# Two conv-style attention layers on one core: heads in pairs, one per half of the matrix rows, and maxima carried in freed position rows

## What is computed

```python
attn = jnp.einsum('bqd,bkd->bqk', q * scale, k)
rel_h = jnp.einsum('bhwc,hkc->bhwk', rq, Rh)
rel_w = jnp.einsum('bhwc,wkc->bhwk', rq, Rw)
attn = attn.reshape(...) + rel_h[..., :, None] + rel_w[..., None, :]
attn = jax.nn.softmax(attn.reshape(Bn * nh, Hh * Ww, Hh * Ww), axis=-1)
out = attn @ v          # then the heads side by side, @ wo + bo
```

## Time and profile before

| what | value |
|---|---|
| runs | 84.46 us median of 3 (84.38 to 84.9) |
| the profiled execution | 84.41 us, its span 82.7 us |
| busy: PE, PEld, DVE, ACT, POOL | 75.9, 61.3, 49.1, 52.7, 6.9 us |
| mean granted TensorE clock | 0.969 |

### The profile page before, as it was taken

How to read it: one execution, slowest core, us unless ns; L and a number is a source line. 1 busy time by engine, 2 the same in 40 slices (tenths; PEclk the granted TensorE clock), 3 DMA queues, 4 the chain that set the end, 5 groups by cost and what they waited for, 6 DMA issues and landing times.

```text
span 82.7 us, 1674 instructions
## 1 busy us (share of the span) xinstructions
PE 75.9 (92%) x656; PEld 61.3 (74%) x656; DVE 49.1 (59%) x128; ACT 52.7 (64%) x100; POOL 6.9 (8%) x22
## 2 busy tenths in 40 slices
PE   4998989998799999999999999999979999999850
PEld 4997879997478876744687989998757885863630
DVE  4476997596977783233167049758777777313210
ACT  6339998999886775743230067799979677471420
POOL 5859100000000000000003000000000000000000
PEclk9999999999999999999995699999999999999995
DMA  1986000000000000000000000000000000000002
GB/s 11 301 196 198 0 0 8 0 0 0 4 0 8 4 0 0 0 0 0 8 0 0 0 0 0 8 0 0 0 0 0 0 0 0 8 0 0 0 0 95
DMA packets 1319, 1.75 MB, mean 21 GB/s; under 512 B 280, under 2 KB 1114, under 8 KB 1312
## 3 DMA queue, kind: packets, MB, share of 16 engines
q1 hardware_dynamic: 1312, 1.66, 7.3%
HBM read 1.46 MB, written 0.20 MB: 20 GB/s over the span
## 4 chain that ended last, share of the span: by engine, by line
PE 79%; DVE 8%; ACT 4%; issue 3%; POOL 1%
PE ps L507 10%; PE ps L632 9%; PE ps L734 9%; PE ps L614 8%; PE ps L591 8%; PE ps L577 7%; PE ps L562 4%; PE ps L714 3%; PE ps L642 3%; ACT qs L271 3%; PE ps L691 2%; PE ps L680 2%; PE ps L534 2%; PE ps L670 2%; PE ps L603 2%
## 5 line engine op out<-in xcount | busy, mean ns | idle before, releaser
L396 DVE TENSOR_REDUCE nm<-ps 128x2 f32<-128x512 f32 x24 | 15.4, 686 | 4.7 <-PE ps L577 4.7
L317 ACT ACTIVATE pt<-ps 128x1024 f32<-128x1024 f32 x12 | 12.3, 1026 | 3.4 <-PE ps L614 3.3
L507 PE MATMUL ps<-busy 128*128 128x128 bf16 x116 | 11.1, 270 | 1.3 <-DVE busy L367 1.0
L271 ACT ACTIVATE qs<-ps 64x512 fp32r<-64x512 f32 x20 | 11.8, 590 | 0.4
L507 PEld LDWEIGHTS ps<-busy 128*128 128x128 bf16 x116 | 9.7, 126 | 2.4 <-DVE busy L367 1.0
L577 PE MATMUL ps<-ks,qs 128*128 128x256 f32 x48 | 8.8, 297 | 0.5 <-DVE nm L396 0.3
L614 PE MATMUL ps<-nmt,ones 4*128 4x256 f32 x48 | 8.8, 302 | 0.0
L591 PE MATMUL ps<-qs,ks 128*128 128x256 f32 x48 | 8.6, 301 | 0.0
L734 PEld LDWEIGHTS ps<-zq,table 128*64 128x64 f32 x128 | 7.9, 138 | 0.7 <-issue 0.5
L734 PE MATMUL ps<-zq,table 128*64 128x48 f32 x128 | 8.1, 216 | 0.2 <-DVE zq L475 0.2
L632 PE MATMUL ps<-pt,va 128*32 128x256 f32 x96 | 8.1, 384 | 0.0
(11 more groups left out here) (88 smaller groups left out, 103.1 us busy)
## 6 DMA issues: line engine op xcount, KB each, us to landing
win<-in_w_in_dram SPq DMA_DIRECT2D x2, 432.0 KB
xt<-in_x_dram SPq DMA_DIRECT2D x1, 192.0 KB, 2.6
wout<-in_w_out_dram SPq DMA_DIRECT2D x2, 96.0 KB
out_dram<-res SPq DMA_DIRECT2D x1, 192.0 KB, 2.0
wout<-in_w_out_dram SPq DMA_DIRECT2D x2, 48.0 KB
rel_raw<-in_rel_dram SPq DMA_DIRECT2D x1, 62.0 KB, 3.5
win<-in_b_in_dram SPq DMA_DIRECT2D x2, 2.2 KB
wout<-in_b_out_dram SPq DMA_DIRECT2D x2, 0.8 KB
```

Source lines behind the costliest of these rows:

```text
L271: return act.activation(dst, src, ACT.Copy, scale=scale)
L317: act.activation(pt[:, p, :, :, :].rearrange("p a k t -> p a (k t)"), ps[:, ST_BANK[p % 2]:ST_BANK[p % 2] + 2, :], ACT.Exp, scale=SCALE[l] ...
L396: dve.tensor_reduce(nm[:, p, a, :], ps[:, S_BANK[a], :].rearrange("p (t k) -> p t k", k=T), AX.X, ALU.max, negate=True).then_inc(max_sb, 1)
L507: mm(ps[:, bank, 0:P], busy[:, :], busy[:, :], start=True, stop=True)
```

## The change

**Rows.** A head's 64 content rows and its 64 position rows no longer share 128 partitions. `qs` and `ks` hold two heads, head a in rows 64a to 64a+63, `rs` the position rows of both, `key_pos` the one-hot pattern twice. A copy is now 128 x 512 or 128 x 256: in each layer eight on ScalarE and two on VectorE. A score is the sum of a content and a position matmul, each 64 rows deep, the two heads in turn in the two row halves and in neighbouring banks.

**Maxima.** GpSimd builds the height table from differences to the first height, which leaves the softmax as it was and makes two position rows of each half free (`key_pos` has ones there). VectorE takes the maxima of a pair at once (128 x 1024); GpSimd splits them into columns 0 and 32 of a 64-column block (`split_maxima`); `turn_max` turns these with 128 columns of weights, and VectorE adds them to the position rows (`max_rows`, `rm`). The transposed scores use `rm` instead of `rs`, so `add_max` and its ones are gone.

**Rest.** The rank-4 products run before the statistics of layer 0, ScalarE copies them out, and GpSimd adds them during layer 0. Height tables are made on GpSimd, width tables on VectorE. `rel` and `lora` are loaded by ScalarE's queue; the output leaves in two halves. Banks and orders are new; `keep_busy` is 28 and 22 in layer 0, 5 and 12 between the layers, and none in the loops.

```diff
+            def split_maxima(l, p):
+                by_tile = nm[:, p, :, :].rearrange("p a t -> p t a")
+                pool.wait_ge(max_sb, PAIRS * l + p + 1)
+                pool.tensor_copy(nmhl[:, p, :, :, 0], by_tile).then_inc(nm_hi, 1)
+                pool.wait_ge(nm_hi, PAIRS * l + p + 1)
+                pool.tensor_tensor(nmhl[:, p, :, :, 32], by_tile, nmhl[:, p, :, :, 0].bitcast(F32),
+                                   ALU.subtract).then_inc(nm_lo, 1)
...
+            for n in range(2):
+                pool.memset(onehot[64 + 32 * n:65 + 32 * n, :, :], 1.0).then_inc(made_onehot, 1)
+            pool.wait_ge(made_onehot, 2)
             inverse_deviation(0)
+            pool.wait_ge(ld_rel, 16)
+            height_differences(0)
+            pool.wait_ge(made_mask, 1)
+            height_table(0)
...
+            for s_ in range(2):
+                pool.wait_ge(ld_win[1], 32)
+                pool.wait_ge(lora_sb, s_ + 1)
+                cols = win[1][0:CH, :, 2 * s_ * C:(2 * s_ + 1) * C]
+                pool.tensor_tensor(cols, lora_w[:, s_, :, :], cols, ALU.add).then_inc(wl_sb, 1)
...
             def maxima(l, p):
-                for a in range(2):
-                    dve.wait_ge(s_ps, NH * l + 2 * p + a + 1)
-                    dve.tensor_reduce(nm[:, p, a, :], ps[:, S_BANK[a], :].rearrange("p (t k) -> p t k", k=T),
...
+                dve.wait_ge(s_ps, PAIRS * l + p + 1)
+                dve.tensor_reduce(nm[:, p, :, :],
+                                  ps[:, S_BANK[p]:S_BANK[p] + 2, :].rearrange("p a (t k) -> p a t k", k=T),
+                                  AX.X, ALU.max, negate=True).then_inc(max_sb, 1)
+            def max_rows(l, p):
+                dve.wait_ge(nmt_ps, PAIRS * l + p + 1)
+                dve.tensor_tensor(rm[:, p, :], ps[:, NM_BANK, 0:T], rs[:, p, :].bitcast(F32),
+                                  ALU.add).then_inc(rm_sb, 1)
...
             def scores_t(l, p):
...
+                for t in range(TT):
+                    for a in range(2):
+                        mm(ps[:, ST_BANK[p] + a, t * T:(t + 1) * T], ks[64 * a:64 * a + 64, p, t * P:(t + 1) * P],
+                           qs[64 * a:64 * a + 64, p, :], start=(t == 0), stop=False, skip_group_check=True)
+                    for a in range(2):
+                        last = mm(ps[:, ST_BANK[p] + a, t * T:(t + 1) * T],
+                                  key_pos[64 * a:64 * a + 64, t * P:(t + 1) * P],
+                                  rm[64 * a:64 * a + 64, p, :], start=False, stop=True, skip_group_check=True)
+                last.then_inc(st_ps, 1)
...
-            def add_max(l, p):
...
             for l in range(LAYERS):
-                if l == 1:
-                    lora_columns(0)
                 keep_busy(BUSY_BEFORE_GROUPS[l])
                 for ic in range(NC):
+                    if l == 0:
+                        if ic == 0:
+                            pe.wait_ge(ld_lora, 16)
+                        lora_columns(ic)
                     group_records(l, ic)
-                if l == 1:
-                    lora_columns(1)
                 keep_busy(BUSY_BEFORE_QK[l])
```

More of the change, by code:

```diff
@@ L487, in _ @@
-                move(l, 1)
-                values(l, 1)
-                move(l, 2)
-                for p in range(PAIRS):
-                    maxima(l, p)
+                                table_w[k][:, part, :, :],
+                                half[:, k, :].bitcast(F32).unsqueeze(2).to_broadcast([P, R, G4]),
+                                head_mask[:, :].unsqueeze(1).to_broadcast([P, R, G4]),
+                                ALU.mult).then_inc(tab_w, 1)
+                for g in range(NG):
+                    z_rest(l, 0, g)
@@ new lines, in _ @@
+                z_rest(l, 1, 0)
+                rr_rest(l, 0)
+                values(l, 0)
+                z_rest(l, 1, 1)
+                for n in range(1, 4):
+                    rr_rest(l, n)
+                z_rest(l, 1, 2)
+                query_move(l, 1)
+                first_relative_move(l)
+                maxima(l, 0)
+                maxima(l, 1)
+                max_rows(l, 0)
+                maxima(l, 2)
+                values(l, 1)
+                max_rows(l, 1)
+                maxima(l, 3)
@@ L565, in relative_rows @@
[L565 to L580 removed]
+                elif g == 1:
+                    pe.wait_ge(k_act, NG * l + 2)
+                else:
+                    pe.wait_ge(r_act, 3 * l + 1)
@@ new lines, in relative_rows @@
+                for u in range(2):
+                    b, c = (R_FIRST[u], 0) if g == 0 else (R_BANK[g], u * T)
+                    for part, (pick, rr) in enumerate(((pick_rh, rr_hi), (pick_rl, rr_lo))):
+                        last = mm(ps[:, b, c:c + T],
+                                  pick[:, 2 * u:2 * u + 2, :].rearrange("p j n -> p (j n)"), rr[:, g, :],
+                                  start=(part == 0 and c == 0), stop=(part == 1), skip_group_check=True)
+                    if u == 1 or g == 0:
+                        last.then_inc(r_ps, 1)
@@ L779, in _ @@
-                probs_v(l, 3)
-                residual(l, 0)
+                scores_t(l, 2)
+                turn_max(l, 3)
+                scores(l, 5)
+                probs_v(l, 0)
+                turn_max(l, 4)
+                scores_t(l, 3)
+                turn_max(l, 5)
+                scores_t(l, 4)
+                scores_t(l, 5)
+                probs_v(l, 1)
+                residual(l, 0)
+                residual(l, 1)
+                turn_out(l, 0)
+                turn_out(l, 1)
```

625 lines of the change are left out of this document (322 added, 303 removed).

## The result

The changed kernel takes **80.28 us** (median of 4 runs, 80.1 to 83.71) where the kernel before takes 84.46: a ratio of 0.949, 95% interval 0.944 to 0.953. The forecast was 78.9 us, between 76.5 and 86.0. The profiled execution took 80.38 us, its span 78.6. Runs of one and the same kernel differ here by the stretches in which TensorE runs at its lower clock, and the ratios leave out the runs that lose most to them; but by their times (84.38 to 84.9) the kernel before had only such runs in this comparison, while in the later series it takes 82.6 to 83.3 us in half of its runs, and against these the changed kernel stands at 0.967 (c1) and 0.966 (e7).

What follows compares the result with a forecast made beforehand. TensorE was taken to bound the kernel. From 84.41 us, loop -4.8, copies -0.8, layer ends +0.8, start +1.3 and between the layers -2.0 sum to -5.5, giving 78.9 us, range 76.5 to 86.0.

Steps and rivals of the forecast that it cites:

- Loop: Loop over pairs in each layer: 8.0 us against 10.4, with depth breaks of 0.21; -2.4 a layer, -4.8 in all.
- GpSimd's split: In the loop: splitting the maxima takes 0.2 us an instruction, 0.4 a pair, covered by VectorE's next maximum of 1.2.
- Copies: Before each layer's loop: eighteen copies become ten, little of it on the path; -0.4 us a layer, bounds 0 and -1.5.
- The height table: Layer 0: GpSimd ends it about 5.5 us after the power, products want it about 5.9 after; up to +1.0 in range.
- End of a layer: ScalarE's exponentials lag behind the last transposed scores; +0.4 us a layer, +0.8 in all; output in two halves costs nothing.
- Start: Rank-4 products ahead of layer 0's statistics delay everything behind them; +1.3 us, bounds +0.8 and +1.9 (late load of `lora`).
- Between the layers: Update products and additions go, 12 dummies replace 24, layer 1's projections start earlier; -2.0 us, bounds -1.0 and -2.1.
- The clock eats the gap: Rival: with fewer dummies between layers, half clock falls on the projections; 80 to 82 us, within a shared chance of 0.14.
- Turns of the halves: Rival: in scores and transposed scores the two row halves take turns instead of overlapping; +9.4, 88.3 us, chance 0.14.

Runs made afterwards that it cites:

- c1: The changed kernel run again without an edit; five runs from 80.14 to 84.16 us, ratio 0.967 to the kernel before.
- e7: Changed kernel with 28 instead of 12 dummy matmuls between layer 0 and layer 1's projections; 79.86 to 81.87 us, ratio 0.966.
- e10: Like e8, with the wait ahead of the first group record bridged by more dummies (38 at the start, 4 between records); 77.19 us, ratio 0.932.
- e3: Changed kernel with the rank-4 products moved behind layer 0's group statistics, 33 dummies ahead and 8 behind; 77.74 us, ratio 0.937.
- e2: Changed kernel with ten dummies in layer 0's wait for the height table, ahead of the third group of small products; 82.04, 82.36, 82.08 and 78.19 us.
- e4: Changed kernel with scores and transposed scores ordered by half, four matmuls of the first head, then four of the second; 82.04 us, ratio 0.966.
- e6: Changed kernel with the start reordered: rank-4 load and products earlier, GpSimd's differences before the power, 28 dummies ahead of both projections; 83.61 us.
- e1: Changed kernel with the first three steps of layer 0's height table on GpSimd ahead of the power; 84.66 us, ratio 1.012.
- e11: Like e10, but with the rank-4 factors on 4 rows, without the zeros; runs from 77.23 to 84.65 us, ratio 0.937.
- e5: Changed kernel with the turn of the maxima in row halves, four matmuls of 64 rows and 64 columns instead of two; 85.69 us.
- e8: Changed kernel with the edits of e3 and e7, VectorE's width tables moved earlier, and rank-4 factors zero-padded to 128 rows; 78.43 us.
- e9: Like e8, but with the rank-4 factors on 4 rows, without the zeros; 80.06 us.

## Why the prediction held, and where it missed

- **The whole.** 80.28 for 78.9, but luck had a part in it. The sum started from an execution with a fall of the clock between the layers, and took what the fall cost for a gain of the change: 24 dummies took 2.67 there, where 28 at full speed take 1.73 (e7), so about 1.2 of the 2.0 (an estimate from these two rows) is the fall. Against 82.6 to 83.3 for the kernel before, the gain is about 2.7 us, half of the 5.5 forecast.
- **Loop.** Right. Both halves start together, a round is 0.12, the breaks are 0.2 wherever 64 rows meet 128; 8.3 for 8.0. Most of the 0.3 missing stands in the chain as one place per layer where VectorE's maximum (1.23) stands ahead of the row addition (0.34) for which the transposed scores wait. "VectorE does the next pair's maximum first, so 1.2 covers 0.4 plus the turn" had that the wrong way round at this one place: the turn was done at 29.24, the addition began only at 29.57, and TensorE waited 0.23 for it.
- **GpSimd's split.** Right: 0.19 and 0.21, never on the chain.
- **Copies.** Too small: -1.11 in layer 1, inside the bounds (0 to -1.5) but well above the 0.4 taken. No run separates the copies from the rest of this stage.
- **The height table.** The step that failed: "Covered, barely; up to +1.0 goes into the range". Working out the table itself from GpSimd's rate was right (1.88 for 2.0), and so was when the products want it (5.9 after the power); but it ended 6.6 after the power instead of 5.5. The steps before it took 2.92 where the sum left 1.5. Of this 0.6 is `diff_lo` beside VectorE's width table, a collision that the sum did not look for; without it they still take 2.25 (e10). What followed was not in the sum for this place: behind the wait of 0.73 the clock stood at 0.50, and the 32 products alone lost 1.6 more. The stage came out 2.2 worse than forecast, more than the whole miss of 1.4. e3, with neither wait nor fall here, is 2.5 us faster; what lowered the clock stays open.
- **End of a layer.** +0.42 where +0.4 was forecast, in layer 0, but by luck: TensorE's last products with v (38.05) waited for no exponential, the last of which ended at 37.0. On the chain stand instead ScalarE's two copies of the output (0.39 each, 39.19 and 41.43), where the chain before has TensorE alone. In layer 1 it gained 0.56; which part of it the output in two halves has was not tried.
- **Start.** +1.16 for +1.3. 0.33 of it is a wait for the load of `lora`, which only the bound had; records of 0.3 for 0.38 and a second product of 0.82 for 1.00 made up for most of it. e3 gave back 0.9 of the 1.16 directly, and more through the table.
- **Between the layers.** -2.03 for -2.0, with the luck named above. And c1 and e2 show the rival "The clock eats the gap" at this very place (5.49 and 4.54 for 2.86) in some runs, and e7 what held it off.
- **Turns of the halves.** Out: e4 did not bring it about even with the order that was to favour it.

## What to carry to other kernels

Ask of every instruction moved to GpSimd what VectorE does beside it: the two can hold each other up by several times an instruction's own length. Count a wait of TensorE twice, once as itself and once as the clock it may cost behind, and fill it; but a fall can come without a wait too. Read the time that a change saves from an execution whose clock did not fall there. Row halves are worth their halved depth whatever the order of their matmuls, but every change of depth between neighbours cost about 0.2 us here.

## What the runs showed of the hardware

- The halves of the rows run apart: matmuls of the second half started with those of the first that stood four places ahead of them (e4).
- Beside GpSimd's instructions of 1.89 to 1.93 us two of VectorE's took 1.97 instead of 0.27 (e6), and two that took 1.09 took 6.36 (e1); GpSimd's own took 1.34 instead of 0.72. VectorE's instructions that read from PSUM kept their length beside them (0.43, 0.55; changed kernel).
- The clock fell behind products 4 rows deep in e11's trace, and not behind the same products padded to 128 rows in e10's: projections 5.38 against 2.86. In the changed kernel's first trace it did not fall behind 4 rows either (2.86).
- Where TensorE stood for 0.23 to 0.42 us near 4.5, the first rise of the clock came late in seven of nine traces (e1, e2, e4, e5, e7, e8, e9), with eight rank-4 products at 2.66 instead of 1.47 (e8, e3); in two it did not (0.33 in the changed kernel, 0.28 in e3). In the three traces with no such wait (c1, e10, e11) it was there.
- The clock fell around a wait of 1.25 us in four of seven traces, and with no wait over 0.1 us behind 64 small products in three (e4, e8, e10).
- The recorded clock can read 1.00 while passes take 0.43 instead of 0.236 (e1), and it does over the first dummies of the changed kernel, 28 in 3.17 us where 22 take 1.40 later. Durations are the better witness.
